# Softmax attention on one Trainium2 core: the product with the values in native fp32 on two column tiles, in place of rounded halves

## The reference, cut to what matters

```
sim  = jnp.einsum('bhid,bhjd->bhij', q, k)          # q already scaled
sim  = jnp.where(causal_mask, -finfo.max, sim + bias)
attn = jax.nn.softmax(sim, axis=-1)
out  = jnp.einsum('bhij,bhjd->bhid', attn, v)       # the product with the values
out  = out.transpose(0, 2, 1, 3).reshape(b, n, h * d) @ Wo + bo
```

## Time and profile before

| what | value |
|---|---|
| time, median of 3 runs | 1695.11 us (1691.37 to 1704.38) |
| the profiled execution | 1696.66 us, of which the trace spans 1694.9 us |
| busy over the span: PE / PEld / DVE / ACT / POOL | 78% / 68% / 67% / 55% / 33% |
| the units of the softmax attention | about 565 to 1370 us of the span |
| mean granted TensorE clock | 0.92 of 2.4 GHz |

### The profile page before, as it was taken

How to read it: one execution, slowest core, us unless ns; L and a number is a source line. 1 busy time by engine, 2 the same in 40 slices (tenths; PEclk the granted TensorE clock), 3 DMA queues, 4 the chain that set the end, 5 groups by cost and what they waited for, 6 DMA issues and landing times. The chain is left out here.

```text
span 1694.9 us, 29601 instructions
## 1 busy us (share of the span) xinstructions
PE 1328.0 (78%) x8596; PEld 1156.7 (68%) x8596; DVE 1129.8 (67%) x3260; ACT 936.9 (55%) x2109; POOL 560.5 (33%) x779
## 2 busy tenths in 40 slices
PE   5778457889944788889888889988889855788990
PEld 4666345778942677778777777877778744677980
DVE  4777646565744577877778777787777745565753
ACT  3444144454512577777767777787777743355540
POOL 1544444353453022221223112232121235343625
PEclk9898769899975899999999999999999967899995
DMA  8950032455723322210222211122220112254854
GB/s 300 420 250 0 1 109 78 134 178 179 212 72 126 71 51 50 50 40 12 51 51 51 51 37 24 41 51 51 51 51 11 42 58 92 91 163 156 250 162 124
DMA packets 89399, 169.12 MB, mean 100 GB/s; under 512 B 13561, under 2 KB 65562, under 8 KB 84764
## 3 DMA queue, kind: packets, MB, share of 16 engines
q1 hardware_dynamic: 76956, 133.64, 26.2%
q0 software_dynamic: 12288, 33.57, 6.4%
HBM read 54.44 MB, written 79.17 MB: 79 GB/s over the span
## 5 line engine op out<-in xcount | busy, mean ns | idle before, releaser
L1854 DVE TENSOR_TENSOR b_pt_lo<-b_pt,b_pt_hi 128x512 fp32r<-128x512 f32 x320 | 215.0, 686 | 100.5 <-ACT b_pt_hi L1735 99.8
L1930 POOL TENSOR_TENSOR b_osum<-b_oa,b_ob 128x256 f32<-128x256 f32 x64 | 46.8, 731 | 619.1 <-ACT b_rb L1749 619.1
L1735 ACT CAST b_pt_hi<-b_pt 128x512 fp32r<-128x512 f32 x320 | 185.4, 584 | 100.5 <-PE b_pt L1587 98.4
L1730 ACT ACTIVATE b_prob<-b_s,b_nmx 128x128 f32<-128x128 f32 (+7 forms) x256 | 189.8, 743 | 87.4 <-DVE b_nmx L1844 86.5
L1587 PE MATMUL b_pt<-all_ident,b_prob 128*128 128x128 f32 x1152 | 192.4, 277 | 19.8 <-ACT b_prob L1730 17.3
L1601 PE MATMUL b_o<-b_pt_hi,b_v 128*128 128x256 f32 x640 | 171.2, 294 | 19.7 <-ACT b_rb L1749 17.4
L1571 PE MATMUL b_s<-b_k_hi,b_q 128*128 128x512 f32 (+1 forms) x384 | 148.2, 390 | 33.9 <-DMA b_k_lo<-b_kn_lo 16.3
L872 POOL DMA_INDIRECT f_w_raw<-xs,f_slots x128 | 122.9, 961 | 150.3 <-DMA xs<-f_eo 82.9
L1601 PE MATMUL b_o<-b_pt_lo,b_v 128*128 128x256 f32 x640 | 163.8, 283 | 0.0
L1587 PEld LDWEIGHTS b_pt<-all_ident,b_prob 128*128 128x128 f32 x1152 | 136.2, 141 | 34.5 <-ACT b_prob L1730 21.3
L1601 PEld LDWEIGHTS b_o<-b_pt_hi,b_v 128*128 128x128 f32 x640 | 121.2, 189 | 44.0 <-ACT b_rb L1749 16.6
(11 more groups left out here) (280 smaller groups left out, 3775.6 us busy)
## 6 DMA issues: line engine op xcount, KB each, us to landing
xs<-a_zeros SPq DMA_DIRECT2D x2, 17408.0 KB, 66.2
f_xg<-xs SPq DMA_DIRECT2D x160, 128.0 KB
xs<-f_eo SPq DMA_DIRECT2D x160, 128.0 KB
b_k_hi<-b_kn_hi SPq DMA_DIRECT2D x64, 256.0 KB, 4.7
b_k_lo<-b_kn_lo SPq DMA_DIRECT2D x64, 256.0 KB, 4.8
f_w_raw<-in_w_ffn SPq DMA_DIRECT2D x20, 384.0 KB, 3.1
out<-all_x SPq DMA_DIRECT2D x8, 512.0 KB, 3.9
all_x<-in_x SPq DMA_DIRECT2D x1, 3072.0 KB, 13.2
```

Source lines behind the costliest of these rows:

```text
L1730: nc.scalar.activation(prob[:, k % 2, t, 0:keys], s_ps[t][:, 0:keys], ACT.Exp, bias=nmx[:, k % 2, t:t + 1], scale=SCALE_B, accum_out=psum_ ...
L1735: nc.scalar.copy(pt_hi[:, 2 * i:2 * i + 2, :], bank_of(k, i)[:]).then_inc(pt_hi_done, 1)
L1854: nc.vector.tensor_tensor(pt_lo[:, 2 * i:2 * i + 2, :], bank_of(k, i)[:], pt_hi[:, 2 * i:2 * i + 2, :].bitcast(F32), ALU.subtract).then_in ...
```

## The change

The values `v` and the transposed probabilities `pt` are kept as plain fp32, in one piece each. The product takes for each key tile and each query tile one native fp32 matmul: 64 stationary columns of `v`, 128 moving query columns. Query tile 0 goes to rows 0 to 63 of `o_ps`, that is to the first 64 columns of the array, query tile 1 to rows 64 to 127. The masked tile is neither transposed nor multiplied. Banks are taken out whole: those of even number by ScalarE, those of odd number by VectorE, with a semaphore each; a bank on the diagonal takes two copies. Of the values, ScalarE takes one key tile and VectorE the other. `out` copies two 64x128 parts and the row sums; GpSimd's addition falls away (its semaphore counts follow), and `ob` stays only for the set-up. A tile of zeros and the wait for it are gone.

```diff
@@ softmax_attention_stage, tiles and semaphores @@
-        zeros = m.sb("zeros", [P, P])
-        v2 = m.sb("v2", [P, BT, 4, 2 * HD_B], F32R)
+        v = m.sb("v", [P, BT, 4, HD_B])
-        pt_hi = m.sb("pt_hi", [P, BT, 2 * P], F32R)
-        pt_lo = m.sb("pt_lo", [P, BT, 2 * P], F32R)
+        pt = m.sb("pt", [P, BT, 2 * P])
-        osum = m.sb("osum", [P, 2 * P])
...
+        def bank_at(k, i):
+            h, u = unit(k)
+            return h * TRI[NU] + TRI[u] + i
+
         def bank_of(k, i):
-            h, u = unit(k)
-            return pt_ps[(h * TRI[NU] + TRI[u] + i) % 2]
+            return pt_ps[bank_at(k, i) % 2]
+
+        def turned_out(eng, b, count):
+
+            if isinstance(b, int) and b * BANKS + count <= 0:
+                return
+            eng.wait_ge(pt_even_done, b * (BANKS // 2) + (count + 1) // 2)
+            if not (isinstance(b, int) and b * BANKS + count == 1):
+                eng.wait_ge(pt_odd_done, b * (BANKS // 2) + count // 2)
...
@@ TensorE @@
                 def turn(b, k, i, fresh):
                     u = unit(k)[1]
-                    nb = banks_before(b, k) + i
                     if i == 0:
                         pe.wait_ge(exp_done, (b * UNITS + k) * 2 + 2)
                     if not fresh:
-                        pe.wait_ge(pt_lo_done, nb - 1)
+                        turned_out(pe, b, bank_at(k, i) - 1)
                     bank = bank_of(k, i)
                     for a in range(2):
                         kt = 2 * i + a
                         for t in range(2):
-                            src = zeros[:] if kt > 2 * u + t else prob[:, k % 2, t, kt * P:(kt + 1) * P]
-                            last = nc.tensor.transpose(bank[:, a, t * P:(t + 1) * P], src, c.ident[:])
+                            if kt <= 2 * u + t:
+                                last = nc.tensor.transpose(bank[:, a, t * P:(t + 1) * P], prob[:, k % 2, t, kt * P:(kt + 1) * P], c.ident[:])
                     last.then_inc(pt_ready, 1)
                 def product(b, k, i, v_number, fresh):
                     u = unit(k)[1]
-                    pe.wait_ge(pt_lo_done, banks_before(b, k) + (i + 1))
+                    turned_out(pe, b, bank_at(k, i) + 1)
                     if i == 0 and not fresh:
                         pe.wait_ge(o_out, (b * UNITS + k) * 3)
                     if v_number is not None:
                         pe.wait_ge(j_done, v_number + 1)
                     for a in range(2):
                         kt = 2 * i + a
-                        for pt in (pt_hi, pt_lo):
-                            last = nc.tensor.matmul(o_ps[:, 0:2 * P], v2[:, kt, unit(k)[0] % 4, :], pt[:, kt, :],
-                                                    start=(kt == 0 and pt is pt_hi), stop=(kt == 2 * u + 1 and pt is pt_lo))
+                        for t in range(2):
+                            if kt <= 2 * u + t:
+                                last = nc.tensor.matmul(o_ps[t * HD_B:(t + 1) * HD_B, 0:P], v[:, kt, unit(k)[0] % 4, :], pt[:, kt, t * P:(t + 1) * P],
+                                                        start=(kt == 0), stop=(kt == 2 * u + t))
...
@@ ScalarE @@
-                        last = nc.scalar.copy(v2[:, 2 * i:2 * i + 2, :, 0:HD_B], bank[:].rearrange("p (t h e) -> p t h e", t=2, h=4))
+                        last = nc.scalar.copy(v[:, 2 * i, :, :], bank[:, 0:D].rearrange("p (h e) -> p h e", h=4))
...
-                def split_pt(b, k, i):
+                def out_pt(b, k, i):
+                    if bank_at(k, i) % 2:
+                        return
                     act.wait_ge(pt_ready, banks_before(b, k) + (i + 1))
-                    nc.scalar.copy(pt_hi[:, 2 * i:2 * i + 2, :], bank_of(k, i)[:]).then_inc(pt_hi_done, 1)
+                    if i == unit(k)[1]:
+                        nc.scalar.copy(pt[:, 2 * i, :], bank_of(k, i)[:, 0, :])
+                        nc.scalar.copy(pt[:, 2 * i + 1, P:], bank_of(k, i)[:, 1, P:]).then_inc(pt_even_done, 1)
+                    else:
+                        nc.scalar.copy(pt[:, 2 * i:2 * i + 2, :], bank_of(k, i)[:]).then_inc(pt_even_done, 1)
...
-                    nc.scalar.copy(oa[rows, u, :], o_ps[0:HD_B, 0:2 * P]).then_inc(o_out, 1)
-                    nc.scalar.copy(ob[rows, u, :], o_ps[HD_B:P, 0:2 * P]).then_inc(o_out, 1)
+                    for t in range(2):
+                        nc.scalar.copy(oa[rows, u, t * P:(t + 1) * P], o_ps[t * HD_B:(t + 1) * HD_B, 0:P]).then_inc(o_out, 1)
                     nc.scalar.copy(rb[rows, u, :], o_ps[rows, 2 * P:]).then_inc(o_out, 1)
...
@@ VectorE @@
-                        last = nc.vector.tensor_tensor(v2[:, 2 * i:2 * i + 2, :, HD_B:], bank[:].rearrange("p (t h e) -> p t h e", t=2, h=4),
-                                                       v2[:, 2 * i:2 * i + 2, :, 0:HD_B].bitcast(F32), ALU.subtract)
+                        last = nc.vector.tensor_copy(v[:, 2 * i + 1, :, :], bank[:, D:].rearrange("p (h e) -> p h e", h=4))
...
-                def split_pt(b, k, i):
-                    dve.wait_ge(pt_hi_done, banks_before(b, k) + (i + 1))
-                    nc.vector.tensor_tensor(pt_lo[:, 2 * i:2 * i + 2, :], bank_of(k, i)[:], pt_hi[:, 2 * i:2 * i + 2, :].bitcast(F32),
-                                            ALU.subtract).then_inc(pt_lo_done, 1)
+                def out_pt(b, k, i):
+                    if bank_at(k, i) % 2 == 0:
+                        return
+                    dve.wait_ge(pt_ready, banks_before(b, k) + (i + 1))
+                    if i == unit(k)[1]:
+                        nc.vector.tensor_copy(pt[:, 2 * i, :], bank_of(k, i)[:, 0, :])
+                        nc.vector.tensor_copy(pt[:, 2 * i + 1, P:], bank_of(k, i)[:, 1, P:]).then_inc(pt_odd_done, 1)
+                    else:
+                        nc.vector.tensor_copy(pt[:, 2 * i:2 * i + 2, :], bank_of(k, i)[:]).then_inc(pt_odd_done, 1)
-                nc.vector.memset(zeros[:], 0.0).then_inc(set_up, 1)
...
@@ GpSimd @@
-                    nc.gpsimd.tensor_tensor(osum[:], oa[:, u, :], ob[:, u, :], ALU.add).then_inc(o_step, 1)
-                    pool.wait_ge(o_step, G * 3 + 1)
-                    nc.gpsimd.tensor_tensor(oa[:, u, :], osum[:], rb[:, u, :], ALU.mult).then_inc(o_step, 1)
-                    pool.wait_ge(o_step, G * 3 + 2)
+                    nc.gpsimd.tensor_tensor(oa[:, u, :], oa[:, u, :], rb[:, u, :], ALU.mult).then_inc(o_step, 1)
```

More of the change, by code:

```diff
@@ L1420, in softmax_attention_stage @@
         s_ready, mx_step, nmx_done, exp_done, rsum_done = (m.sem(s) for s in ("s_ready", "mx_step", "nmx_done", "exp_done", "rsum_done"))
-        pt_ready, pt_hi_done, pt_lo_done, pv_done = (m.sem(s) for s in ("pt_ready", "pt_hi_done", "pt_lo_done", "pv_done"))
+        pt_ready, pt_even_done, pt_odd_done, pv_done = (m.sem(s) for s in ("pt_ready", "pt_even_done", "pt_odd_done", "pv_done"))
         o_out, o_step, o_done = m.sem("o_out"), m.sem("o_step"), m.sem("o_done")
@@ L1654, in _ @@
                 pe.wait_ge(w_lo_done, 3)
-                pe.wait_ge(set_up, 2)
+                pe.wait_ge(set_up, 1)
                 for i in range(BC * DB, len(PRO)):
@@ L1775, in body @@
                                 if what == "h":
-                                    split_pt(b, k, i)
+                                    out_pt(b, k, i)
                                 elif more:
@@ L1929, in combine @@
                         pool.wait_ge(o_done, G)
-                    nc.gpsimd.tensor_tensor(osum[:], oa[:, u, :], ob[:, u, :], ALU.add).then_inc(o_step, 1)
-                    pool.wait_ge(o_step, G * 3 + 1)
-                    nc.gpsimd.tensor_tensor(oa[:, u, :], osum[:], rb[:, u, :], ALU.mult).then_inc(o_step, 1)
-                    pool.wait_ge(o_step, G * 3 + 2)
+                    nc.gpsimd.tensor_tensor(oa[:, u, :], oa[:, u, :], rb[:, u, :], ALU.mult).then_inc(o_step, 1)
+                    pool.wait_ge(o_step, G * 2 + 1)
                     if y_number is not None:
@@ L1938, in combine @@
                     nc.gpsimd.tensor_scalar(o_hi[:, cols], oa[:, u, :], 1.0, 1.0, ALU.mult, ALU.mult).then_inc(o_step, 1)
-                    pool.wait_ge(o_step, G * 3 + 3)
+                    pool.wait_ge(o_step, G * 2 + 2)
                     nc.gpsimd.tensor_tensor(o_lo[:, cols], oa[:, u, :], o_hi[:, cols].bitcast(F32), ALU.subtract).then_inc(o_done, 1)
```

## The result

On one chip, by turns, the changed kernel took 1690.37 us (median of 20 runs, 1683.43 to 1700.09) and the kernel before 1697.74 (20 runs, 1687.7 to 1707.02). The ratio is 0.9956, interval 0.994 to 0.9973. The time lies in the range of the forecast, but the gain is 7 us in place of 27, and within the 1% that was called no change.

What follows compares the result with a forecast made beforehand. TensorE, busy 703 of 805 us in the attention units and idle 102, was taken as the bound. Product +19, zeros -14 and waits -32 sum to -27 on 1696.66: 1669, so 1668 us; range 1640 to 1735.

Steps and rivals of the forecast that it cites:

- The native matmul: Product on TensorE: two column tiles side by side, five slots of 0.107 us a bank, 171 us, 19 more.
- the bound of four slots: Product on TensorE: a bank without the extra slot at either end takes four slots, 137 us, 15 less.
- rival 2: TensorE around the product: 512 tile-shape changes at 0.09 us cost +37, 1705 us; at 0.16, 1734; chance 0.16.
- The loads: Product's weight loads on TensorE: expected to fit beside the matmuls; at the upper end they add 34 us.
- Rival 1: Product on TensorE: column tiles run one after another, +94 in place of +19, 1727 us; chance 0.28.
- Rival 3: TensorE's waits: tiles overlap but exponentials and transfers hold it as before, +5, 1701 us; chance 0.10.
- The copies: Copies of banks, values and out: ScalarE -120 us of 586, VectorE -115 of 615, paying only through TensorE's waits.
- The waits: TensorE's waits for values, out and exponentials, banks, and the keys' delay: together -32 us, bounds 0 and -48.
- the 8 taken for them: Ends of the 16 pairs: keys no longer queue behind a bank's halves, about 0.5 us each, -8 us.
- the prediction's signs: Wait before a pair's first scores: longer than 1.7 us if the forecast is right, shorter if tiles run one after another.
- The pinned stretch: End of each of 16 pairs: lasts as long as the keys' transfers; TensorE savings become wait, added work swallowed up to 1.7 us.
- The zeros: TensorE's 128 transposes of zeros go, at 0.11 us each: -14 us on its path.

Runs made afterwards that it cites:

- extra_64: Kernel before the change plus one native matmul per product bank, 64 stationary columns (one column tile), 128 moving; 1812.94 us, 1.0666 of the kernel before.
- two_step_copies: Changed kernel, but ScalarE copies every bank whole, then VectorE subtracts into an unread tile, product waiting for both; 1.0056 of the kernel before.
- k_early: Changed kernel with a pair's second k job one unit earlier, exchanged with the second q job; 1679.28 us, 0.9883 of the kernel before.
- no_zeros: Kernel before the change with the masked tile neither transposed nor multiplied, rounded halves kept; 1695.68 us, 0.9994 of the kernel before.
- extra_128: Kernel before the change plus one native matmul per product bank, 128 stationary and 128 moving columns; 1734.86 us, 1.022 of the kernel before.
- one_block_turn_first: Changed kernel with a unit's first transposes, then its whole product, then the other transposes; 1690.45 us, 0.9958 of the kernel before.
- turn_first_k_early: Changed kernel with first transposes, whole product, other transposes per unit, and the second k job one unit earlier; 1696.47 us, 0.9997 of the kernel before.
- before_k_early: Kernel before the change with a pair's second k job one unit earlier, exchanged with the second q job; 1696.07 us, 0.9982 of the kernel before.

## Why the prediction was wrong, by its steps

**The native matmul (+19; measured +47): the step that failed.** It asked how the tiles overlap and gave no price to the way in and out. (Of the 47, 4 are the lower clock's.) Both halves were off. The overlap was better than taken: -6 inside the runs, near the bound of four slots. And each run of product records pays 0.13 us going in and 0.15 coming out. The sum set these at nothing and left them to rival 2, at 0.16 chance and 0.09 to 0.16 us a change; `extra_64` measures 0.12. The rival's mechanism was right, and the place to carry it was the sum. Its time (1705 to 1734) came out too high because it was put on top of the +19, and 1690 lies in the range by luck: the overlap that nobody had counted on gave back half of the ends. With what was measured: 1669 - 25 (overlap) + 53 (ends) - 3 (transposes) - 3 (scores, jobs) + 1 (waits) = 1692; the profiled execution took 1687.85, with 5 us less outside the stage, about what such executions differ by.

The nearest rows had been seen: 0.09 us between transposes with 128 and with 8 rows. They were read as "whether that is a change of tile they do not say", and the term went to zero instead of to the nearest row. 0.09 x 512 = 46 is near the 53 that were measured; with it the sum would have read 1714, too high by what the overlap then gave back. The measured 0.13 and 0.15 are nearer to the 0.16 that the prediction had as the most.

The Trainium skill (TensorEngine Tiling (Array Packing), Key Properties) says that changing the tiling mode drains TensorE. The trace agrees: the distance into and out of a run of 64-column records is 0.25 us where it was 0.11 to 0.12. Another rule of the Trainium skill, that weight loads overlap matmuls in flight only across row groups (TensorE: Matmul & The Clock Gate, Part 3: Packing small matmuls), is contradicted by this case for column tiles, which share all rows: the six loads of the run at 950.43 lie between 950.42 and 950.83, so the last one starts at about 950.69, while the run's first record, 0.32 us long, is still in flight.

**The loads (+34 at the upper end):** not seen. A slot inside a run stays at 0.107 us with two loads of 64 columns in each.

**The clock: in no term.** Some 7 us, by 25.3 us busy at 0.50 where it was 11.5. The waits that stayed before the pairs are what stands ahead of it (last section).

**Rival 1, tiles one after another:** refuted by 0.060 us a record. **Rival 3, waits that do not shrink:** refuted, idle time fell by 30.5.

**The copies (-120 and -115 us):** right, 117 and 105 in the busy times. Their worth, through waits, was 14 us for the banks' part by `two_step_copies`, out of a term of 32 for all.

**The waits (-32; measured -30.5): right in sum, wrong in parts, so the sum is luck.** The values' waits fell from 14.8 to 9.2, not to nothing: the copies of both engines run at once, but each wait still lasts 0.6 us. Those for exponentials and `rb` before product and transposes fell from 34.7 to 22.0, 13 us where 7.5 were taken. A wait for the query projection on VectorE, 9.0 before, fell to 1.4, which the forecast did not name. The 28 us before pairs' first scores stayed 28: the 8 taken for them did not come, nor did they grow as the prediction's signs had it.

**The pinned stretch: right as a mechanism, not in what it costs.** VectorE finished the keys at 955.33 and the scores came at 962.72 before. After, these are 947.28 and 954.67:

```profile
946.59 0.69 DVE L1829 TENSOR_TENSOR b_kn_lo<-b_j,b_kn_hi 128x512 fp32r<-128x512 f32 x1
```

Both are 7.39 us, with another product on TensorE in between. The wait that is put down to `b_prob` at 954.67 belongs to the transfer: `k_early` only exchanges the keys' job with a q job, and it went. What hung on it is some 10 us, by the pair of kernels with keys early. The forecast had it as time swallowed; but with the stretch gone, idle time only fell by 2 to 4 us in either kernel, and most of the 10 are the clock's.

**The zeros (-14):** right as work (-17), but `no_zeros` shows that in the kernel before such work alone buys nothing: 15 of its 18 us became waits, and the lower clock took some 8. The forecast took work off TensorE at full value, and waits off it beside that; the two are not independent. Work added comes through at half to nearly full (38 of 68 us in `extra_128`; 78 of 88 more in `extra_64`). Work removed turned into waits (nothing of 18 in `no_zeros` and of 21 at the upper clock in `one_block_turn_first`), with the keys early too (`turn_first_k_early`). By which dependence exactly the exponentials then come too late is told by the waits' rows only; no experiment moved them alone.

## What to carry to other kernels

Price the way into and out of a tile shape by the number of times that a kernel alternates, before pricing what the tiles save; here 512 changes at 0.12 us took back more than half of what two tiles side by side gave (41 to 53 us of 77). When an engine waits at several places in turn, count what a change removes from it once, against the waits behind it, and look for the one wait of fixed length: the edit that moved the keys' job by one unit was worth more than the change itself, and only together with it. It took away long waits, not waiting; so read the granted clock of both traces before a difference is put down to waits or work. The 220 us taken from engines that do not bind are worth only the waits that they shorten: 14 us for the banks' part, where it was measured.

## What the runs showed of the hardware

Records of two column tiles start 6 to 8 ns apart where their matmuls alternate in the queue, and 13 or 14 where two of one tile come first. Only the second pair of a run comes 0.16 us after the first instead of 0.107; whether that is part of the price of the change was not tried.

The granted clock fell after longer waits. At 954.67 a wait of 1.74 us ends, and from 956 to 958 the clock is at 0.50, the 1.2 GHz level: there eight records take 1.12 us in place of 0.66, four transposes from 955.83 1.12 in place of 0.60. Between 575 and 1350 us of the span:

| kernel | waits of TensorE of 1.6 us or more | falls of the clock | us at 0.50 |
|---|---|---|---|
| before | 11 | 2 | 6.8 |
| `before_k_early` | 3 | 3 | 10.2 |
| `no_zeros` | 13 | 7 | 23.9 |
| changed | 10 | 6 | 20.5 |
| changed, second profile | 12 | 7 | 23.9 |
| `k_early` | 1 | 1 | 3.4 |
| `turn_first_k_early` | 26 | 10 | 34.1 |

In the changed kernel's two profiles, in `k_early` and in `turn_first_k_early` each fall comes during such a wait or within 1.7 us of its end; the three of `before_k_early` come after shorter waits. Why 11 long waits lower the clock twice in the kernel before and 10 six times in the changed one is not shown. No experiment varied the clock alone: that it carries 7 us of the change and 10 of `k_early` is worked out from the traces, as half of the time in which TensorE is busy at 0.50.
